# A selective-scan kernel: GpSimd weighs the last token block of 20 of 32 states, TensorE sums them in PSUM, three decay banks

## The chip, the cores and the metric

The kernel runs on one core of a Trainium2 chip. The metric is the device time of one execution in microseconds (us). Matmuls run on TensorE (PE; its weight loads are PEld), scans and sums on VectorE (DVE), table functions and copies out of PSUM on ScalarE (ACT), products in SBUF on GpSimd (POOL), and SyncE (SP) issues the DMAs.

## The reference

Eight sequences of 1024 tokens with 512 features. The result is `x + mamba(layernorm(x)) + ffn(layernorm(x))`; the FFN with its FP4 rounding comes first and is not touched. What matters is the selective scan of the other branch, with 1024 channels d and 16 states s:

```python
def step(h, inp):
    xt, dtt, Bt, Ct = inp
    dA = jnp.exp(dtt[:, :, None] * A[None])
    h = h * dA + (dtt * xt)[:, :, None] * Bt[:, None, :]
    y = jnp.einsum('bds,bs->bd', h, Ct)
    return (h, y)
...
y = y + xc * D_param[None, None, :]
y = y * _silu(z)
return y @ W_out
```

## The kernel before

`phase_b` works through 16 chunks of 512 tokens, two to a sequence; all engines run the same list of slots for every chunk (`over_chunks`), with a hardware loop whose body is two chunks. Channels lie on partitions in two halves of four tiles of 128. A chunk has 32 states k: 0 to 15 are the 16 states of the first half, 16 to 31 those of the second. A state has four tiles j; tile n = 4k + j, 128 to a chunk. I call the time of one state a slot.

For tile n, ScalarE computes the decay exp(dt * A) into the PSUM bank `decay[n % 4]` (L1058), after the scan that read this bank before. GpSimd computes v = u * B into `v[k % 2]` (`drive`, L920), with row B broadcast over partitions by a DMA (`load_b`). VectorE scans along the 512 tokens into `h[k % 2]` (`hs`, L1099). The second chunk of a sequence starts from carried states (`carry`), the first from zero; their scans are listed apart. When the four scans of a state are done, TensorE turns its four blocks t of 128 tokens one after the other so that tokens lie on partitions (`turn_states`, L1216, four transposes of 128 x 128 each into `ht[n % 2]`), and VectorE adds each, times C of its tokens (one number per partition), to `acc[g][:, t, :]` (`add_state`, L1113). TensorE turns tile n in place n + 4 of its list and VectorE adds it in place n + `LAG` = n + 5, so VectorE alternates: scan n, addition n - 5. The first scan of state k waits until state k - 2 is turned, for its buffer.

The rest is spread over the list by hand. `MM` gives the place from which TensorE works on each other product (`ip`, `cv`, `z`, `ssm`, `ct`, `xd`, `yt`, `wo`), 4/3 units a tile; a unit is one K-slice, two matmul instructions of 512 columns. `ACT_AT` gives ScalarE's copies and functions after decay n; the SiLUs need a change of the function table and back (`silu_xc` at 31, 38, 68, 76, `silu_z` at 4 and 87). `DVE_AT` has eight additions of a residual tile (`rtb`, L1085), `POOL_AT` by slot the products y2 = acc * silu(z) (L929) and the last steps of softplus and u = dt * x (`sp`, `du`; L933, L937). `SP_AT` has the DMAs. GpSimd's v of state k goes ahead of the scans by up to two states (it waits for the scan of state k - 2 that read the same buffer). `c_now` is copied once a chunk. Eight PSUM banks are in use: four `decay`, two `ht`, two `mm`.

Of the kernel before, what the change touches and what calls it, by code (L numbers as in the profile page):

```python
# [636 lines left out]
def phase_b(nc, ctx, xnt, res, ssm_d, tap_d, ident, out, W_in, conv_w, conv_b, W_x, A_log, D_param, dt_bias, W_out):  # L637
# [25 lines left out]
    LAG = 5  # L663
    assert ND == 2 * GD and NT == 4 and D == CL and GW == 512 and KC == 4
# [10 lines left out]
    w_in, w_out = sb("w_in", [P, KH, 2 * DI]), sb("w_out", [P, ND, D])  # L675
# [15 lines left out]
    b_rep = [sb(f"b_rep{p}", [P, CL]) for p in range(4)]  # L691
    dt_rep = sb("dt_rep", [P, CL])
# [7 lines left out]
    decay = [psum(f"decay{p}", [P, CL]) for p in range(4)]  # L700
# [16 lines left out]
    b_loaded = [sem(f"b_loaded{p}") for p in range(4)]  # L717
# [17 lines left out]
    for i, part_ in enumerate(MM):  # L735
        for unit in range(UNITS[part_[1]]):
            while room == 0 or place < part_[0]:
# [29 lines left out]
    POOL_AT = {1: [("y2", 1, 0), ("y2", 1, 1)], 2: [("y2", 1, 2), ("y2", 1, 3)],  # L767
# [4 lines left out]
    SP_AT = {2: [("load", 1, 0), ("load", 1, 1)], 5: [("tap", 2)], 7: [("tap", 3)], 8: [("store", 1, 0)],  # L772
             9: [("store", 1, 1), ("load", 1, 2)], 10: [("tap", 4), ("load", 1, 3)], 11: [("tap", 5)], 13: [("store", 1, 2)],
             15: [("store", 1, 3)], 16: [("tap", 6)], 17: [("tap", 7), ("x_in",)], 19: [("tap", 0)],
             20: [("load", 0, 0), ("load", 0, 1)], 21: [("tap", 1)], 23: [("ssm",)], 25: [("store", 0, 0)],
             26: [("store", 0, 1), ("load", 0, 2)], 27: [("load", 0, 3)], 28: [("store", 0, 2)], 29: [("store", 0, 3)],
             31: [("x_z",)]}

# [47 lines left out]
    def _(sp):  # L826
# [24 lines left out]
        sp.dma_start(w_out[:, :, :], W_out.rearrange("(k p) n -> p k n", p=P)).then_inc(w_out_loaded, 16)  # L851
# [8 lines left out]

        def move(c, what, *args):
            o = whose(c, what, *args[:1])
            if what == "tap":
                i, = args
                o = c.plus(1 if i >= 2 else 2)
                if o.exists(NC):
                    load_taps(o, i)
            elif what == "x_in":
# [25 lines left out]
        def part(c):  # L894
            for k in range(SLOTS):
                for what in SP_AT.get(k, ()):
                    move(c, *what)
                if k + 3 < SLOTS:
                    if c.exists(NC):
                        load_b(c, k + 3)  # L900
                elif c.plus(1).exists(NC):
                    load_b(c.plus(1), k + 3 - SLOTS)
# [6 lines left out]
    def _(pool):  # L909
# [11 lines left out]

        def extra(c, what, g, j):
# [3 lines left out]
            if what == "y2":  # L926
                wait(pool, z_ready, o.at(4, 2 * g + j // 2 + 1))
                wait(pool, summed, o.at(128, 64 * g + 61 + j))
# [10 lines left out]
        def part(c):  # L939
            for k in range(SLOTS):  # L940
                if c.exists(NC):
                    drive(c, k)
                for what in POOL_AT.get(k, ()):
                    extra(c, *what)
# [4 lines left out]
    def _(act):  # L949
# [101 lines left out]
        def part(c):  # L1051
            for n in range(4 * SLOTS):
                if c.exists(NC):
                    g, s, j = n // 64, n // 4 % NS, n % 4
                    if s == 0:
                        wait(act, dt_ready, c.at(8, 4 * g + j + 1))
                    wait(act, scanned, c.at(128, n - 3))
                    nc.scalar.activation(decay[n % 4][:, :], dt[g][:, j, :], ACT.Exp,  # L1058
                                         scale=a_neg[:, GD * g + j, s:s + 1]).then_inc(decay_ready, 1)
# [12 lines left out]
    def _(dve):  # L1072
# [15 lines left out]
        def scan(c, n):  # L1088
            g, s, j = n // 64, n // 4 % NS, n % 4
            k = n // 4  # L1090
            if j == 0:
                wait(dve, turned, c.at(128, 4 * (k - 2) + 4))
                if c.second and k < 2:
                    wait(dve, carried, c.in_firsts(32, 2 * NS - 1 + k))
                elif not c.second and k >= 2:
                    wait(dve, carried, c.in_firsts(32, k - 1))
            wait(dve, v_ready, c.at(128, n + 1))
            wait(dve, decay_ready, c.at(128, n + 1))
            nc.vector.tensor_tensor_scan(h[k % 2][:, j, :], decay[n % 4][:, :], v[k % 2][:, j, :],  # L1099
# [3 lines left out]
        def add_state(c, n):  # L1103

            g, s, t = n // 64, n // 4 % NS, n % 4
            if s == 0:
# [3 lines left out]
            else:  # L1110
                wait(dve, summed, c.at(128, n - 3))
            wait(dve, turned, c.at(128, n + 1))
            nc.vector.scalar_tensor_tensor(out=acc[g][:, t, :], in0=ht[n % 2][:, :, :].rearrange("p j d -> p (j d)"),  # L1113
                                           scalar=c_now[:, t, s:s + 1], in1=acc[g][:, t, :],
                                           op0=ALU.mult, op1=ALU.add).then_inc(summed, 1)

        def part(c):
            for n in range(4 * SLOTS):
# [3 lines left out]
                if before.exists(NC):  # L1122
                    add_state(before, m)
                if n == LAG - 1 and c.exists(NC):
                    wait(dve, summed, c.at(128, 0))
# [8 lines left out]
    def _(pe):  # L1134
        pe.wait_ge(w_in_x_loaded, 16)

        def products(c, n, unit):
# [61 lines left out]
            else:  # L1199
                (g, t), j = args, unit  # L1200
                if first:
                    if isinstance(c.q, int) and c.c == 0 and (g, t) == (0, 0):
                        pe.wait_ge(w_out_loaded, 16)
                    wait(pe, yt_copied, o.at(8, 4 * g + t + 1))
                made, done = nc.tensor.matmul(bank[:, :], yt[t % 2][:, j, :], w_out[:, GD * g + j, :],  # L1205
# [4 lines left out]
        def turn_states(c, n):  # L1210

            k, t = n // 4, n % 4
            wait(pe, scanned, c.at(128, 4 * k + 4))
            wait(pe, summed, c.at(128, n - 1))
            for j in range(GD):
                last = nc.tensor.transpose(ht[n % 2][:, j, :], h[k % 2][:, j, t * P:(t + 1) * P], ident[:, :])  # L1216
            last.then_inc(turned, 1)

        def part(c):
            for n in range(4 * SLOTS):  # L1220
                before, m = (c, n - 4) if n >= 4 else (c.plus(-1), n + 4 * SLOTS - 4)
                if before.exists(NC):
                    turn_states(before, m)
                for i, unit in units_at[n]:
# [48 lines left out]
```

## Time and profile before

| | |
|---|---|
| median of 3 runs | 5823.27 us (5817.52 to 5824.12) |
| the profiled execution | 5821.8 us |
| its span, first to last instruction | 5819.3 us |
| PE busy | 4983.0 us (86%) |
| VectorE busy | 5030.1 us (86%) |
| ScalarE busy | 2782.2 us (48%) |
| GpSimd busy | 3629.1 us (62%) |
| chain that ended last, by engine | DVE 30%, PE 13%, issue 13%, ACT 6%, POOL 4% |

Busy shares are over the whole span; the scans begin at 1937.58 us. In the timeline rows the first number is the start in us, the second the length in us, and x is how many equal instructions were merged; square brackets give the idle time ahead and what ended it. The rows of the lines have busy us and mean ns of one.

### The profile page before, as it was taken

What the parts mean: (1) busy time and instruction counts of PE and PEld (TensorE: products, weight loads), DVE (VectorE), ACT (ScalarE), POOL (GpSimd) and SP (SyncE); (2) the same over time, 40 slices, a digit from 0 to 9 for tenths busy, and PEclk for the clock granted to TensorE, in tenths of its full rate; (3) what the DMA queues carried; (4) which work ended last, traced back from release to release, by engine and by line L of the source; (5) the groups of instructions that cost most, each with busy time, mean ns of one, the idle gap of its engine ahead of it and who ended that gap; (6) DMA issues with size and microseconds to landing.
All of it is one profiled execution on the core that took longest, in us unless ns stands there. A gap on an engine that the chain in (4) does not pass through costs nothing.

```text
span 5819.3 us, 78029 instructions
## 1 busy us (share of the span) xinstructions
PE 4983.0 (86%) x21764; PEld 3148.0 (54%) x21764; DVE 5030.1 (86%) x6343; ACT 2782.2 (48%) x4591; POOL 3629.1 (62%) x2810
## 2 busy tenths in 40 slices
PE   1799999999998788888888888888888888888867
PEld 1688888888885344444444444444444444444444
DVE  7667666676662699999999999999999999999998
ACT  1111111111111666666666666666666665666654
POOL 4333333333331687878778788787877878878785
PEclk9999999999999899999999999999999999999968
DMA  2111111111112222222222222222222222222211
GB/s 74 33 40 43 42 41 43 40 43 40 43 40 79 65 78 71 73 73 67 75 71 75 71 65 79 68 75 73 66 74 71 75 70 67 76 71 75 61 57 49
DMA packets 211700, 362.55 MB, mean 62 GB/s; under 512 B 26208, under 2 KB 58976, under 8 KB 207216
## 3 DMA queue, kind: packets, MB, share of 16 engines
q1 hardware_dynamic: 211312, 358.17, 19.8%
q8 instruction: 147, 2.41, 0.2%
q14 instruction: 241, 1.97, 0.1%
HBM read 287.80 MB, written 70.29 MB: 62 GB/s over the span
## 4 chain that ended last, share of the span: by engine, by line
DVE 30%; PE 13%; issue 13%; ACT 6%; POOL 4%; DVEq 1%; DMA 0%; ACTq 0%; SPq 0%; POOLq 0%
DVE hs L1099 18%; DVE acc L1113 11%; PE ht L1216 5%; PE mm L1205 4%; POOL v L920 3%; ACT decay L1058 3%; PE mm L1156 2%; PE mm L1165 2%; DVEq L795 1%; POOL dt L933 1%; DVE rtb L1085 1%; ACT L1067 1%; ACT L983 1%; PE mm L1173 1%; ACT xc L983 1%
## 5 line engine op out<-in xcount | busy, mean ns | idle before, releaser
L920 POOL TENSOR_TENSOR v<-u,b_rep 128x512 f32<-128x512 f32 x2048 | 2578.2, 1273 | 698.0 <-DVE hs L1099 688.6
L1216 PEld LDWEIGHTS ht<-ident,hs 128*128 128x128 f32 x8192 | 957.4, 147 | 1883.7 <-DVE acc L1113 907.1
L1216 PE MATMUL ht<-ident,hs 128*128 128x128 f32 x8192 | 1362.7, 292 | 629.4 <-DVE acc L1113 577.6
L1058 ACT ACTIVATE decay<-dt,a_neg 128x512 f32<-128x512 f32 x2048 | 1377.3, 686 | 600.5 <-DVE hs L1099 575.7
L1113 DVE SCALAR_TENSOR_TENSOR acc<-ht,c_now,acc 128x512 f32<-128x512 f32 x2048 | 1479.9, 723 | 24.0 <-PE ht L1216 23.7
L1099 DVE TENSOR_TENSOR_SCAN hs<-decay,v 128x512 f32<-128x512 f32 x1024 | 1238.3, 1209 | 128.6 <-POOL v L920 105.5
L1099 DVE TENSOR_TENSOR_SCAN hs<-decay,carry,v 128x512 f32<-128x512 f32 x1024 | 1301.3, 1271 | 13.7 <-ACT decay L1058 8.1
L490 ACT ACTIVATE sg<-gate 128x512 f32<-128x512 f32 (+1 forms) x192 | 108.1, 563 | 1334.1 <-PE up L536 1334.1
L1156 PE MATMUL mm<-x_in,w_in 128*128 128x512 f32 x1024 | 526.3, 620 | 20.7 <-DMA x_in<-xnt_d 17.3
L1205 PE MATMUL mm<-w_out,yt 128*128 128x512 f32 x1024 | 537.5, 625 | 0.3 <-ACT yt L1021 0.3
L1173 PE MATMUL mm<-w_in,x_z 128*128 128x512 f32 x1024 | 520.8, 611 | 0.0
L1165 PE MATMUL mm<-xb,tap_diag 128*128 128x512 f32 (+3 forms) x1024 | 501.2, 594 | 2.7 <-ACT xc L978 1.9
L106 POOL TENSOR_TENSOR h<-h,h_small 128x1408 f32<-128x1408 f32 x64 | 166.2, 2597 | 440.3 <-DVE h_small L100 440.3
L151 POOL TENSOR_TENSOR h<-h,h_small 128x1408 f32<-128x1408 f32 x64 | 166.3, 2599 | 335.2 <-DVE h L145 335.2
L435 DVE TENSOR_TENSOR rt<-down,rt 128x512 f32<-128x512 f32 x64 | 44.3, 692 | 323.9 <-PE down L536 323.9
L534 PE MATMUL gate<-gu,xqt 128*128 128x512 f32 (+1 forms) x768 | 301.4, 392 | 5.4 <-DVE xqt L426 5.4
L536 PE MATMUL gate<-gu,xqt 128*128 128x512 f32 (+1 forms) x768 | 289.7, 377 | 0.0
L535 PE MATMUL gate<-gu,xqt 128*128 128x512 f32 (+1 forms) x768 | 289.7, 377 | 0.0
L534 PE MATMUL up<-gu,xqt 128*128 128x512 f32 (+1 forms) x768 | 288.8, 376 | 0.0
L535 PE MATMUL up<-gu,xqt 128*128 128x512 f32 (+1 forms) x768 | 288.6, 376 | 0.0
L536 PE MATMUL up<-gu,xqt 128*128 128x512 f32 (+1 forms) x768 | 288.5, 376 | 0.0
L534 PE MATMUL down<-wd,hqt 128*128 128x512 f32 x704 | 285.1, 405 | 2.5 <-DVE hqt L418 2.5
(122 smaller groups left out, 6948.0 us busy)
## 6 DMA issues: line engine op xcount, KB each, us to landing
b_rep<-ssm_d SPq DMA_DIRECT2D x512, 256.0 KB, 3.4
tap_diag<-tap_d SPq DMA_DIRECT2D x128, 256.0 KB, 3.0
rtb<-res_d SPq DMA_DIRECT2D x128, 256.0 KB, 4.1
xt<-in_L_attn_x SPq DMA_DIRECT2D x64, 256.0 KB, 2.8
xnt_d<-xntb SPq DMA_DIRECT2D x64, 256.0 KB, 2.7
rt<-in_L_attn_x SPq DMA_DIRECT2D x64, 256.0 KB, 2.6
res_d<-rt SPq DMA_DIRECT2D x64, 256.0 KB, 2.0
x_in<-xnt_d SPq DMA_DIRECT2D x16, 1024.0 KB, 4.8
```

What stands on the lines that cost most here:

```text
L534: nc.tensor.matmul(out, left_hi, right_hi, start=(k == 0), stop=False)
L535: nc.tensor.matmul(out, left_hi, right_lo, start=False, stop=False)
L536: last = nc.tensor.matmul(out, left_lo, right_hi, start=False, stop=(k == len(pairs) - 1))
L920: nc.gpsimd.tensor_tensor(v[k % 2][:, j, :], u[g][:, j, :], b_rep[k % 4][:, :], ALU.mult).then_inc(v_ready, 1)
L1058: nc.scalar.activation(decay[n % 4][:, :], dt[g][:, j, :], ACT.Exp, scale=a_neg[:, GD * g + j, s:s + 1]).then_inc(decay_ready, 1)
L1099: nc.vector.tensor_tensor_scan(h[k % 2][:, j, :], decay[n % 4][:, :], v[k % 2][:, j, :], carry[:, s, GD * g + j:GD * g + j + 1] if c.secon ...
L1113: nc.vector.scalar_tensor_tensor(out=acc[g][:, t, :], in0=ht[n % 2][:, :, :].rearrange("p j d -> p (j d)"), scalar=c_now[:, t, s:s + 1], i ...
L1156: made, done = nc.tensor.matmul(bank[:, :], w_in[:, k, i * P:(i + 1) * P], x_in[:, k, :], start=first, stop=last), ip_done
L1165: made, done = nc.tensor.matmul(bank[:, skip:], tap_diag[i % 2][:, tap, :], xb[i % 2][:, tap + skip:tap + CL], start=first, stop=last), cv ...
L1173: made, done = nc.tensor.matmul(bank[:, :], x_z[:, k, t * P:(t + 1) * P], w_in[:, k, DI + g * GW:DI + (g + 1) * GW], start=first, stop=las ...
L1205: made, done = nc.tensor.matmul(bank[:, :], yt[t % 2][:, j, :], w_out[:, GD * g + j, :], start=first, stop=last), wo_done
L1216: last = nc.tensor.transpose(ht[n % 2][:, j, :], h[k % 2][:, j, t * P:(t + 1) * P], ident[:, :])
```

## The change

A set of 20 of the 32 states is `WEIGHED`. For these the last token block (t = 3, `LT`) isn't added by VectorE: GpSimd multiplies the block of `h` by C (row C broadcast by a new DMA, `load_c`) into its own buffer `hw` (`weigh`, after the v of two states later), and TensorE transposes the products into one PSUM bank `yw`, accumulating over the states (`turn_weighed`, two places after where the block was turned). VectorE adds `yw` to the sum once for each half (`add_weighed`), and y2 of the last block waits for it. The bank comes from the decays: three instead of four (`decay_freed` says which scan frees one; the ring begins anew with each chunk). The first scan of state k waits for the weighing of state k - 2 too. For SBUF, `w_out` holds one half and is loaded twice a chunk. GpSimd's other work and the counts of the semaphores are moved accordingly.

```diff
+    LT = NT - 1
+    WEIGHED = (2, 3, 4, 6, 8, 10, 12, 13, 14, 15, 16, 17, 18, 19, 22, 23, 24, 25, 26, 30)
+    LATE = 2
...
-    w_in, w_out = sb("w_in", [P, KH, 2 * DI]), sb("w_out", [P, ND, D])
+    w_in, w_out = sb("w_in", [P, KH, 2 * DI]), sb("w_out", [P, GD, D])
...
+    c_rep = [sb(f"c_rep{p}", [P, P]) for p in range(4)]
+    hw = [sb(f"hw{p}", [P, GD, P]) for p in range(2)]
...
-    decay = [psum(f"decay{p}", [P, CL]) for p in range(4)]
+    decay = [psum(f"decay{p}", [P, CL]) for p in range(3)]
+    yw = psum("yw", [P, GD, P])
...
-    POOL_AT = {1: [("y2", 1, 0), ("y2", 1, 1)], 2: [("y2", 1, 2), ("y2", 1, 3)],
-               6: [("sp", 1, 0), ("du", 1, 0)], 7: [("sp", 1, 1), ("du", 1, 1)], 8: [("sp", 1, 2), ("du", 1, 2)],
-               9: [("sp", 1, 3), ("du", 1, 3)], 22: [("y2", 0, 0), ("y2", 0, 1)], 23: [("y2", 0, 2), ("y2", 0, 3)],
-               29: [("sp", 0, 0), ("du", 0, 0)], 30: [("sp", 0, 1), ("du", 0, 1)],
-               31: [("sp", 0, 2), ("du", 0, 2), ("sp", 0, 3), ("du", 0, 3)]}
-    SP_AT = {2: [("load", 1, 0), ("load", 1, 1)], 5: [("tap", 2)], 7: [("tap", 3)], 8: [("store", 1, 0)],
+    POOL_AT = {2: [("y2", 1, 0), ("y2", 1, 1)], 3: [("y2", 1, 2), ("y2", 1, 3)], 7: [("sp", 1, 0), ("du", 1, 0)],
+               9: [("sp", 1, 1), ("du", 1, 1)], 11: [("sp", 1, 2), ("du", 1, 2)], 13: [("sp", 1, 3), ("du", 1, 3)],
+               22: [("y2", 0, 0), ("y2", 0, 1)], 23: [("y2", 0, 2), ("y2", 0, 3)], 29: [("sp", 0, 0), ("du", 0, 0)],
+               30: [("sp", 0, 1), ("du", 0, 1)], 31: [("sp", 0, 2), ("du", 0, 2), ("sp", 0, 3), ("du", 0, 3)]}
+    SP_AT = {2: [("w_out", 1), ("load", 1, 0), ("load", 1, 1)], 5: [("tap", 2)], 7: [("tap", 3)], 8: [("store", 1, 0)],
...
-             15: [("store", 1, 3)], 16: [("tap", 6)], 17: [("tap", 7), ("x_in",)], 19: [("tap", 0)],
+             15: [("store", 1, 3), ("w_out", 0)], 16: [("tap", 6)], 17: [("tap", 7), ("x_in",)], 19: [("tap", 0)],
...
+    NW = len(WEIGHED)
+    weigh_no = {k: i for i, k in enumerate(WEIGHED)}
+    weighed_until = [sum(k < NS * g for k in WEIGHED) for g in range(3)]
+    add_no = {m: i for i, m in enumerate((k, t) for k in range(SLOTS) for t in range(NT)
+                                         if t != LT or k not in weigh_no)}
+    ADDS = len(add_no)
...
+    def sums(c, k, t):
+        return c.at(ADDS, max(i for (a, b), i in add_no.items() if b == t and a <= k) + 1)
+    def states_done(c, k, of, per):
+        if k < 0:
+            return c.at(per, sum(i <= k + SLOTS for i in of) - per)
+        return c.at(per, sum(i <= k for i in of))
+    def decay_freed(c, n):
+        return c.at(128, n - 2) if n >= 3 else c.at(128, (126, 127, 125)[n] + 1 - 128)
...
-        sp.dma_start(w_out[:, :, :], W_out.rearrange("(k p) n -> p k n", p=P)).then_inc(w_out_loaded, 16)
...
+        def load_c(c, k):
+            w, row = weigh_no[k], k % NS
+            wait(sp, weighed, c.at(NW, w - 3))
+            sp.dma_start(c_rep[w % 4][:, :],
+                         ssm_rows(c, row, row + 1)[:, LT * P:].broadcast_to([P, P])).then_inc(c_loaded[w % 4], 16)
...
         def move(c, what, *args):
...
+            elif what == "w_out":
+                g, = args
+                o = c.plus(-g)
+                if o.exists(NC):
+                    wait(sp, wo_done, o.at(8, 4 * g))
+                    sp.dma_start(w_out[:, :, :], w_out_rows[:, GD * g:GD * g + GD, :]).then_inc(w_out_loaded, 16)
...
+                if c.exists(NC) and k in weigh_no:
+                    load_c(c, k)
...
                         load_b(c, k + 3)
...
+        def weigh(c, k):
+            w = weigh_no[k]
+            wait(pool, c_loaded[w % 4], c.at(4 * NW, 16 * (w // 4) + 16))
+            wait(pool, w_turned, c.at(NW, w - 1))
+            wait(pool, scanned, c.at(128, 4 * k + 4))
+            nc.gpsimd.tensor_tensor(hw[w % 2][:, :, :], h[k % 2][:, :, LT * P:],
+                                    c_rep[w % 4][:, :].unsqueeze(1).broadcast_to([P, GD, P]),
+                                    ALU.mult).then_inc(weighed, 1)
         def extra(c, what, g, j):
...
             if what == "y2":
...
-                wait(pool, summed, o.at(128, 64 * g + 61 + j))
+                if j == LT:
+                    wait(pool, yw_added, o.at(2, g + 1))
+                else:
+                    wait(pool, summed, sums(o, NS * g + NS - 1, j))
                 nc.gpsimd.tensor_tensor(sz[:, j, :], acc[g][:, j, :], sz[:, j, :], ALU.mult).then_inc(y2_ready, 1)
...
                     drive(c, k)
+                done, m = (c, k - 2) if k >= 2 else (c.plus(-1), k + SLOTS - 2)
+                if done.exists(NC) and m in weigh_no:
+                    weigh(done, m)
...
-                    wait(act, scanned, c.at(128, n - 3))
-                    nc.scalar.activation(decay[n % 4][:, :], dt[g][:, j, :], ACT.Exp,
+                    wait(act, scanned, decay_freed(c, n))
+                    nc.scalar.activation(decay[n % 3][:, :], dt[g][:, j, :], ACT.Exp,
                                          scale=a_neg[:, GD * g + j, s:s + 1]).then_inc(decay_ready, 1)
...
             if j == 0:
-                wait(dve, turned, c.at(128, 4 * (k - 2) + 4))
+                wait(dve, turned, states_done(c, k - 2, [i for i, _ in add_no], ADDS))
+                wait(dve, weighed, states_done(c, k - 2, weigh_no, NW))
...
             wait(dve, v_ready, c.at(128, n + 1))
...
-            nc.vector.tensor_tensor_scan(h[k % 2][:, j, :], decay[n % 4][:, :], v[k % 2][:, j, :],
+            nc.vector.tensor_tensor_scan(h[k % 2][:, j, :], decay[n % 3][:, :], v[k % 2][:, j, :],
...
         def add_state(c, n):
...
-            g, s, t = n // 64, n // 4 % NS, n % 4
-            if s == 0:
+            g, s, k, t = n // 64, n // 4 % NS, n // 4, n % 4
+            if s == 0 or (t == LT and all((NS * g + i, t) not in add_no for i in range(s))):
...
-                wait(dve, summed, c.at(128, n - 3))
-            wait(dve, turned, c.at(128, n + 1))
-            nc.vector.scalar_tensor_tensor(out=acc[g][:, t, :], in0=ht[n % 2][:, :, :].rearrange("p j d -> p (j d)"),
+                wait(dve, summed, sums(c, k - 1, t))
+            wait(dve, turned, sums(c, k, t))
+            nc.vector.scalar_tensor_tensor(out=acc[g][:, t, :], in0=ht[add_no[k, t] % 2][:, :, :].rearrange("p j d -> p (j d)"),
...
+        def add_weighed(c, g):
+            wait(dve, w_turned, c.at(NW, weighed_until[g + 1]))
+            wait(dve, summed, sums(c, NS * g + NS - 1, LT))
+            nc.vector.tensor_tensor(acc[g][:, LT, :], yw[:, :, :].rearrange("p j d -> p (j d)"), acc[g][:, LT, :],
+                                    ALU.add).then_inc(yw_added, 1)
...
         def part(c):
...
                     scan(c, n)
-                if before.exists(NC):
+                if before.exists(NC) and (m // 4, m % 4) in add_no:
...
+                for g in range(2):
+                    owner = c if g == 0 else c.plus(-1)
+                    if n == (64 * (g + 1) + LAG + 4) % 128 and owner.exists(NC):
+                        add_weighed(owner, g)
...
-                    wait(dve, summed, c.at(128, 0))
+                    wait(dve, summed, c.at(ADDS, 0))
...
-                    if isinstance(c.q, int) and c.c == 0 and (g, t) == (0, 0):
-                        pe.wait_ge(w_out_loaded, 16)
+                    wait(pe, w_out_loaded, o.at(32, 16 * g + 16))
...
-                made, done = nc.tensor.matmul(bank[:, :], yt[t % 2][:, j, :], w_out[:, GD * g + j, :],
+                made, done = nc.tensor.matmul(bank[:, :], yt[t % 2][:, j, :], w_out[:, j, :],
...
+            if (k, t) not in add_no:
+                return
             wait(pe, scanned, c.at(128, 4 * k + 4))
-            wait(pe, summed, c.at(128, n - 1))
+            wait(pe, summed, c.at(ADDS, add_no[k, t] - 1))
             for j in range(GD):
-                last = nc.tensor.transpose(ht[n % 2][:, j, :], h[k % 2][:, j, t * P:(t + 1) * P], ident[:, :])
+                last = nc.tensor.transpose(ht[add_no[k, t] % 2][:, j, :], h[k % 2][:, j, t * P:(t + 1) * P], ident[:, :])
             last.then_inc(turned, 1)
+        def turn_weighed(c, k):
+            g, w = k // NS, weigh_no[k]
+            wait(pe, weighed, c.at(NW, w + 1))
+            if w == weighed_until[g]:
+                wait(pe, yw_added, c.at(2, g))
+            for j in range(GD):
+                last = nc.tensor.matmul(yw[:, j, :], hw[w % 2][:, j, :], ident[:, :], is_transpose=True,
+                                        start=(w == weighed_until[g] and j == 0),
+                                        stop=(w == weighed_until[g + 1] - 1 and j == GD - 1))
+            last.then_inc(w_turned, 1)
...
         def part(c):
...
                     turn_states(before, m)
+                done, k = (c, n - 7 - LATE) if n >= 7 + LATE else (c.plus(-1), n + 4 * SLOTS - 7 - LATE)
+                if done.exists(NC) and k % 4 == 0 and k // 4 in weigh_no:
+                    turn_weighed(done, k // 4)
...
```

## Rows read from the trace of the kernel before

**Rows 1.** The page: the span.
```profile
span 5819.3 us, 78029 instructions
```

**Rows 2.** Busy us (count) of PE, PEld, DVE, ACT, POOL, clock, DMA in a stretch.
```profile
2647.00:3131.00 484.00, 410.18 (x1712) 214.44 (x1712) 473.45 (x531) 308.70 (x500) 380.90 (x305) 0.97 0.23 72
```

**Rows 3.** Lines of the page.
```profile
L920 POOL TENSOR_TENSOR v<-u,b_rep 128x512 f32<-128x512 f32 x2048 | 2578.2, 1273 | 698.0 <-DVE hs L1099 688.6
...
L1113 DVE SCALAR_TENSOR_TENSOR acc<-ht,c_now,acc 128x512 f32<-128x512 f32 x2048 | 1479.9, 723 | 24.0 <-PE ht L1216 23.7
L1099 DVE TENSOR_TENSOR_SCAN hs<-decay,v 128x512 f32<-128x512 f32 x1024 | 1238.3, 1209 | 128.6 <-POOL v L920 105.5
```

**Rows 4.** Timeline of DVE, a chunk that starts at zero.
```profile
3513.18 1.21 DVE L1099 TENSOR_TENSOR_SCAN hs<-decay,v 128x512 f32<-128x512 f32 x1
3514.31 0.72 DVE L1113 SCALAR_TENSOR_TENSOR acc<-ht,c_now,acc 128x512 f32<-128x512 f32 x1
3514.96 1.21 DVE L1099 TENSOR_TENSOR_SCAN hs<-decay,v 128x512 f32<-128x512 f32 x1
```

**Rows 5.** Timeline of DVE, a chunk with carried states.
```profile
3617.41 1.27 DVE L1099 TENSOR_TENSOR_SCAN hs<-decay,carry,v 128x512 f32<-128x512 f32 x1
...
3619.24 1.27 DVE L1099 TENSOR_TENSOR_SCAN hs<-decay,carry,v 128x512 f32<-128x512 f32 x1
```

**Rows 6.** Timeline around tile 43.
```profile
3457.99 0.68 DVE L1085 TENSOR_TENSOR rtb<-mm,rtb 128x512 f32<-128x512 f32 x1
3457.99 0.72 ACT L1011 ACTIVATE xs<-xc,dpar 128x512 f32<-128x512 f32 x1 [5.13 <-PE mm L1191]
...
3459.39 1.22 DVE L1099 TENSOR_TENSOR_SCAN hs<-decay,v 128x512 f32<-128x512 f32 x1 [0.72 <-ACT decay L1058]
```

**Rows 7.** Waits of DVE from 1937 to 5800: total us, times, longest.
```profile
DVE acc L1113 <- PE ht L1216: 23.7, 14, 3.8
DVE hs L1099 <- ACT decay L1058: 22.6, 28, 1.8
DVE hs L1099 <- PE ht L1216: 13.3, 20, 1.7
DVE rtb L1085 <- PE mm L1205: 12.6, 15, 2.3
```

**Rows 8.** Timeline of the first scans.
```profile
1936.28 9.85 POOL L920 TENSOR_TENSOR v<-u,b_rep 128x512 f32<-128x512 f32 x8
1937.58 6.11 DVE L1099 TENSOR_TENSOR_SCAN hs<-decay,v 128x512 f32<-128x512 f32 x5 [105.49 <-POOL v L920]
```

**Rows 9.** Lines of POOL in the first 1900 us.
```profile
L151 POOL TENSOR_TENSOR xq<-xq,q_small 128x512 f32<-128x512 f32 x64 | 68.0, 1063 | 196.5 <-DVE xq L145 196.5
...
L106 POOL TENSOR_TENSOR w_t<-w_raw,w_small 128x512 f32<-128x512 f32 x22 | 30.4, 1382 | 75.7 <-DVE w_small L130 71.9 <-DVE w_small L100 3.7
```

**Rows 10.** Timeline of PE (matmuls), tiles with one and with two units.
```profile
3522.68 0.60 PE L1216 MATMUL ht<-ident,hs 128*128 128x128 f32 x4
...
3523.98 0.63 PE L1216 MATMUL ht<-ident,hs 128*128 128x128 f32 x4
...
3526.22 1.88 PE L1173 MATMUL mm<-w_in,x_z 128*128 128x512 f32 x4
3527.94 0.60 PE L1216 MATMUL ht<-ident,hs 128*128 128x128 f32 x4
```

**Rows 11.** Timeline from decay 87 to decay 88.
```profile
3532.16 0.69 ACT L1058 ACTIVATE decay<-dt,a_neg 128x512 f32<-128x512 f32 x1 [1.08 <-DVE hs L1099]
...
3535.90 2.50 POOL L929 TENSOR_TENSOR sz<-acc,sz 128x512 f32<-128x512 f32 x2 [2.44 <-ACT sz L1000]
...
3538.09 2.53 ACT L1058 ACTIVATE decay<-dt,a_neg 128x512 f32<-128x512 f32 x4
```

**Rows 12.** DMA issues: count, KB each, median us to landing.
```profile
b_rep<-ssm_d SPq DMA_DIRECT2D x512, 256.0 KB, 3.4
...
w_out<-in_L_attn_W_out SPq DMA_DIRECT2D x1, 2048.0 KB, 19.9
```

More of the change, by code:

```diff
@@ L716, in phase_b @@
     rt_loaded, rt_stored = ([sem(f"{s}{p}") for p in range(2)] for s in ("rtb_loaded", "rtb_stored"))
-    b_loaded = [sem(f"b_loaded{p}") for p in range(4)]
+    b_loaded, c_loaded = ([sem(f"{s}_loaded{p}") for p in range(4)] for s in "bc")
+    weighed, w_turned, yw_added = sem("weighed"), sem("w_turned"), sem("yw_added")
     v_ready, decay_ready, scanned, turned, summed, carried = (
@@ L777, in phase_b @@
              31: [("x_z",)]}
+    NW = len(WEIGHED)
[4 more added lines that the diff above has]
+    ADDS = len(add_no)
+    assert ADDS % 2 == 0 and NW % 4 == 0
+    def sums(c, k, t):
[6 more added lines that the diff above has]
+        return c.at(128, n - 2) if n >= 3 else c.at(128, (126, 127, 125)[n] + 1 - 128)
     def bank_of(*task):
@@ L850, in _ @@
         sp.dma_start(w_in[:, :, DI:2 * DI], w_in_rows[:, :, DI:2 * DI]).then_inc(w_in_z_loaded, 16)
-        sp.dma_start(w_out[:, :, :], W_out.rearrange("(k p) n -> p k n", p=P)).then_inc(w_out_loaded, 16)
+        w_out_rows = W_out.rearrange("(k p) n -> p k n", p=P)
         def load_b(c, k):
```

## The prediction

> **What bounds the kernel now.** Read the span first [rows 1], then a stretch of the steady phase [rows 2], the table of lines [rows 3], VectorE's timeline [rows 4 to 6] and last its waits [rows 7]. The first 1937.6 us of the span are the FFN and the first projections, and the change does not touch them. From there VectorE runs 2048 scans and 2048 additions. In 484 us of this phase (one pair of chunks) it is busy for 473.45, GpSimd for 380.90, and TensorE's clock is granted at 0.97 of its upper level, 2.4 GHz [rows 2]. The timeline says what a tile costs on VectorE: a scan starts 1.13 us before the addition behind it, the next scan 0.65 us after that; each overlaps the end of the one ahead by 0.08 us [rows 4]. So a tile takes 1.77 us in a chunk that starts at zero and 1.83 us in one that starts from carried states [rows 4, 5]. Per chunk that is 128 x 1.77 = 226.6 or 128 x 1.83 = 234.2 us. The eight additions of a residual take 0.60 each (0.68 less the overlap [rows 6]) and the copy of C 0.7, so 232.1 and 239.7; eight of each are 3774 us. VectorE's waits after the first scan add 23.7 + 22.6 + 13.3 + 12.6 = 72.2 us [rows 7]. With the first 1937.6 us and a tail of 26 us this gives 5810, 0.2% off the span of 5819.3 [rows 1]. **VectorE's own work is the path, and a VectorE instruction that disappears is worth its pitch, not its busy time.**
>
> **Part by part.** The sum is made against the profiled execution, 5821.8 us; the median of the runs is 1.5 us above it, and I add that at the end. Tile n is 4k + j of state k, a slot is the time of one state.
>
> *Removed: 20 of 128 additions a chunk.* An addition is 723 ns busy [rows 3] but its pitch between two scans is 1.77 - 1.13 = 0.64 us. 320 of them: **-204.8 us**, if a scan behind a scan starts after 1.13 us as an addition does. The trace has scans in a row only at the very start: five in 6.11 us, a pitch of 1.225, while GpSimd delivered their inputs at (9.85 - 1.26) / 7 = 1.227 [rows 8]; they were paced by GpSimd, so the pitch lies between 1.13 and 1.22. I take 1.13, because every other VectorE instruction here overlaps its forerunner; the other end costs 320 x 0.08 = 26 us and stays in the range.
>
> *Added on VectorE: one addition of the bank yw to each half's sum.* 32 x 0.60 (priced as the residual's addition [rows 6]) = **+19.2 us**. It waits for the last accumulating transpose, two tiles back, and GpSimd's y2 of the last block waits for it; that y2 sits a state behind, so neither is late.
>
> *Moved to GpSimd: 20 products a chunk.* Price between 1.06 us (a product with a broadcast operand) and 1.38 us [rows 9]; I take 1.27, the line next to it on the same data [rows 3]. GpSimd's busy time per chunk goes from 190.5 to 190.5 + 25.4 = 215.9 us against some 233 for VectorE. A weighed slot has five GpSimd operations at a pitch of 1.23 to 1.24, 6.2 us, against VectorE's 3 x 1.77 + 1.13 = 6.44. A product can end 2.0 us after the start of a slot at the earliest (its state's last scan ends, one v, the product) and is due when the next slot starts, so GpSimd may be 4.4 us late. The slots with two softplus or y2 operations take 7.5 us against 7.1; the last has four of them and takes 10. From slot 24 (0.8 us before due) over 25 to 31 this goes -1.6, -1.9, -2.7, -3.5, -2.5, -2.1, +0.8, and the one due at the next chunk's start is met by 0.1 us. Nothing in the sum, but no room either. One rule speaks against such a move: the Trainium skill, GPSIMD Engine Reference, section Engine selection, puts elementwise work on VectorE, since GpSimd is about twice as slow with two inputs. The rows say 1.27 against 0.72, 1.8 times; by the page's factor the product would be 1.44 us and GpSimd's chunk 219 us, still under VectorE's.
>
> *TensorE.* As many transposes as before (80 a chunk accumulate into yw, two tiles later). A tile with one product unit takes 1.30 us, with two 1.72 + 0.44 = 2.16 [rows 10], on average 1.59; VectorE's weighed tile is 6.44 / 4 = 1.61. TensorE may be late by 2.0 us against VectorE before an addition waits. It nearly becomes a second bound; 0.5 us a chunk for jitter. Against that, a scan of state k that waited for the last transpose of state k - 2 is now released one tile earlier where that state is weighed (states 0, 25 and 26, where most of these waits lie): **-10** of the 13.3 us [rows 7].
>
> *Three decay banks.* ScalarE may be two tiles and a bit ahead instead of three: it loses one pitch, 1.77 us, of cover wherever it stops for long. Its longest stop is the SiLU of z with two table loads at tile 87: decay 87 starts at 3532.16, decay 88 ends at 3538.09 + 0.63, 6.6 us later [rows 11]. With four banks the start is the end of scan 83; with three, the end of scan 84, and scan 88 is due 3 x 1.77 + 1.13 - 1.21 = 5.2 us after that: 1.4 us late. The same shift delays y2, which idles 2.44 us there already [rows 11]; that is in the slack above. 1.45 and 1.25 us in the two kinds of chunk, **+21.6**. The other stops with table loads are 3.9 us; in weighed slots 3.7 are covered: +0.4 in the even chunks, +3. At tile 43 a scan already waits 0.72 us for a decay behind a copy that waits for TensorE [rows 6]; the accumulating transposes of state 8 come one tile ahead of it (0.44) and the tile before is shorter: +0.8 a chunk, **+13**. At a chunk's start the ring begins anew, and decays 0 and 1 may start only after scans 126 and 127: ready 0.8 us later, due 2.3 us later. ScalarE's other copies wait for TensorE and come three tiles behind it, which three banks still allow.
>
> *SyncE's queue.* 20 rows of C a chunk, issued two slots ahead (13 us) against 3.4 us for a row of B; half of W_out twice a chunk, issued 2.3 slots (15 us) ahead, where all of it took 19.9 us once [rows 12]. Each stands ahead of B rows that have three slots. Hidden; if a C row were late it would hold GpSimd and, within 4.4 us, every scan.
>
> Sum: -204.8 + 19.2 - 10 + 21.6 + 3 + 13 + 8 (jitter) = -150. 5821.8 - 150 = 5671.8; plus 1.5: **5673 us**.
>
> **Rivals.** (1) *Scans in a row at 1.21 us:* +26, 5699; chance 0.12. (2) *GpSimd becomes the bound:* it decides once GpSimd has more than 233 - 216 = 17 us of idle a chunk that it can't make up (before, it idled for 51, nearly all on scans). For: no spare in slots 24 to 31 and a y2 that waits for ScalarE. Against: each step above meets its date. With 20 us of such idle, 3 x 16 = +48: 5721; chance 0.09. (3) *TensorE becomes the bound in weighed slots:* from a mean of 1.61 us a tile. At 1.65, 0.04 x 4 x 320 = +51: 5724; chance 0.09. (4) *Slower: the ring of decays.* Each place where ScalarE stops pays the full lost pitch, 1.77 us, on VectorE. The gain without ScalarE's terms is 196 us, 12.2 a chunk, so it decides from seven such places; ScalarE has six table blocks and some thirty copies that wait for TensorE, and with ten paid places the time is 5823 - 196 + 283 = 5910. For: ScalarE is busy for 309 of 484 us [rows 2] and a bank is its only cover. Against: scans waited for decays only 28 times, 22.6 us in all [rows 7]. Chance 0.07, and 0.01 for a smaller loss. (5) *The change does nothing:* the bank can't be summed in time and the stalls meet the gain; 5823, chance 0.03.
>
> **How the numbers follow.** The forecast has 0.59. Its own bounds: nothing new stalls, -204.8 + 19.2 - 13.3 = -199, 5624; all stalls twice as dear, 5720. Rivals 1 to 3 reach 5750 with the longer scan pitch on top, so the range is 5620 to 5750. What a measurement here can tell from no change is 0.2%, 12 us. Faster 0.59 + 0.12 + 0.09 + 0.09 = 0.89, same 0.03, slower 0.08.
>
> **What would show it.** VectorE's group of additions 1728 instead of 2048 at 723 ns, its busy time down by 26 us in a pair of chunks; scans in a row 1.13 apart; waits on decays up from 22.6 to about 55 to 60 us, most at tile 88; waits on transposes at a state's first scan down to a few us; no wait on products of GpSimd. If scans wait for v or the weighed buffer, rival 2; if additions wait for transposes in slots 14 to 21, rival 3; if waits on decays pass 150 us, rival 4. The prediction is wrong if a pair of chunks takes less than 458 or more than 476 us.

## The result and the profile after

| | before | after |
|---|---|---|
| median of the runs | 5821.25 us | 5686.77 us (5684.53 to 5689.05) |
| ratio | | 0.9768, 95% interval 0.9757 to 0.978 |
| span of the profiled execution | 5819.3 us | 5684.8 us |
| VectorE busy | 5030.1 us | 4871.6 us |
| GpSimd busy | 3629.1 us | 3984.9 us |

The change takes 134.5 us off the span, 2.3% of the time. The forecast was 5673 us in a range of 5620 to 5750; the gain was forecast at 150 us. From the second pair of chunks on, a pair takes 466 to 470 us, within the 458 to 476 us that the prediction gave.

The lines of the page that answer to [rows 1] and [rows 3], busy us and mean ns of one, then the idle time ahead:

```profile
span 5684.8 us, 79958 instructions
...
L963 POOL TENSOR_TENSOR v<-u,b_rep 128x512 f32<-128x512 f32 x2048 | 2555.2, 1274 | 201.9 <-DVE hs L1159 188.0
...
L1159 DVE TENSOR_TENSOR_SCAN hs<-decay,v 128x512 f32<-128x512 f32 x1024 | 1232.3, 1216 | 152.3 <-POOL v L963 108.4
L1159 DVE TENSOR_TENSOR_SCAN hs<-decay,carry,v 128x512 f32<-128x512 f32 x1024 | 1293.3, 1275 | 26.7 <-ACT decay L1117 17.5
L1173 DVE SCALAR_TENSOR_TENSOR acc<-ht,c_now,acc 128x512 f32<-128x512 f32 x1728 | 1262.1, 730 | 11.9 <-PE ht L1288 11.4
...
L971 POOL TENSOR_TENSOR hw<-hs,c_rep 128x512 f32<-128x512 f32 x320 | 407.7, 1274 | 6.2 <-DVE hs L1159 6.2
```

There are 320 additions less, and GpSimd has 320 products at 1274 ns, the price of v. Its idle time ahead of v fell from 698 us to 202: the slack went into the products. From the list of all lines, the new addition of yw and the copy of C:

```profile
L1181 DVE TENSOR_TENSOR acc<-yw,acc 128x512 f32<-128x512 f32 x32 | 21.8, 681 | 0.1
...
L1198 DVE COPY c_now<-c_next 128x64 f32<-128x64 f32 x16 | 39.9, 2494 | 1.6
```

The second row is the surprise. This copy was there before, and its sixteen took 10.8 us in all; its row of before, and of after, as min/median/max ns:

```profile
L1127 DVE COPY c_now<-c_next x16: 168/718/1351, 1943.6 to 5557.5; 128x64 f32<-128x64 f32 x16
```
```profile
L1198 DVE COPY c_now<-c_next x16: 170/2624/3759, 1941.5 to 5434.3; 128x64 f32<-128x64 f32 x16
```

The same stretch as [rows 2] (busy us of PE, PEld, DVE, ACT, POOL, clock, DMA) and VectorE's waits after the first scan. As in [rows 7], the last four additions of a residual, in the final 20 us, are left out:

```profile
2647.00:3131.00 484.00, 413.58 (x1777) 227.11 (x1775) 471.06 (x512) 325.32 (x519) 442.00 (x358) 0.98 0.28 88
```
```profile
DVE hs L1159 <- ACT decay L1117: 43.7, 39, 1.8
DVE hs L1159 <- PE ht L1288: 18.7, 17, 1.6
DVE rtb L1144 <- PE mm L1275: 16.8, 19, 2.3
DVE acc L1173 <- PE ht L1288: 11.4, 21, 1.0
DVE hs L1159 <- POOL hw L971: 5.8, 4, 1.9
DVE hs L1159 <- issue: 2.2, 1, 2.2
DVE hs L1159 <- POOL v L963: 1.6, 1, 1.6
```

VectorE is the path as before; GpSimd is busy for 442 of 484 us instead of 381. The waits sum to 100.2 us against 72.2. The account of the span: removed additions 320 x 0.64 = -204.8; yw +19.2; the copy of C 39.9 us now against 10.8, +29; waits +28.0; the first scan 2.1 us earlier (1935.48). That makes -130.6 of the measured -134.5; the last 4 us stay without a name.

### The profile page after: what moved, and what is told of

It is laid out like the page before. It is cut to its first block, busy times and chain, and to the rows that moved or that the text cites. A ratio compares the mean times of both kernels' runs of the same rounds, so it can differ in the third digit from the quotient of the medians.

```text
span 5684.8 us, 79958 instructions
## 1 busy us (share of the span) xinstructions
PE 4886.1 (86%) x21764; PEld 3186.2 (56%) x21764; DVE 4871.6 (86%) x6055; ACT 2821.3 (50%) x4591; POOL 3984.9 (70%) x3130
## 3 DMA queue, kind: packets, MB, share of 16 engines
q8 instruction: 142, 2.33, 0.2%
## 4 chain that ended last, share of the span: by engine, by line
DVE 23%; issue 18%; POOL 11%; PE 7%; ACT 7%; DVEq 1%; DMA 0%; POOLq 0%; ACTq 0%; SPq 0%
DVE hs L1159 14%; POOL v L963 8%; DVE acc L1173 8%; ACT decay L1117 3%; PE mm L1275 2%; PE ht L1288 2%; PE mm L1227 1%; DVEq L823 1%; POOL dt L989 1%; POOL sz L985 1%; ACT L1042 1%; POOL hw L971 1%; ACT xc L1042 1%; DVE rtb L1144 1%; PE mm L1244 1%
## 5 line engine op out<-in xcount | busy, mean ns | idle before, releaser
L963 POOL TENSOR_TENSOR v<-u,b_rep 128x512 f32<-128x512 f32 x2048 | 2555.2, 1274 | 201.9 <-DVE hs L1159 188.0
L1117 ACT ACTIVATE decay<-dt,a_neg 128x512 f32<-128x512 f32 x2048 | 1399.5, 688 | 1061.0 <-DVE hs L1159 1033.6
L1288 PEld LDWEIGHTS ht<-ident,hs 128*128 128x128 f32 x6912 | 827.8, 146 | 1503.4 <-issue 629.3
L1288 PE MATMUL ht<-ident,hs 128*128 128x128 f32 x6912 | 1127.5, 288 | 500.8 <-DVE acc L1173 318.6
L1173 DVE SCALAR_TENSOR_TENSOR acc<-ht,c_now,acc 128x512 f32<-128x512 f32 x1728 | 1262.1, 730 | 11.9 <-PE ht L1288 11.4
L1275 PE MATMUL mm<-w_out,yt 128*128 128x512 f32 x1024 | 517.2, 612 | 43.5 <-ACT xb L1027 26.4
L1244 PE MATMUL mm<-w_in,x_z 128*128 128x512 f32 x1024 | 507.0, 603 | 0.0
L971 POOL TENSOR_TENSOR hw<-hs,c_rep 128x512 f32<-128x512 f32 x320 | 407.7, 1274 | 6.2 <-DVE hs L1159 6.2
```

Of the source, the lines that this page charges most:

```text
L963: nc.gpsimd.tensor_tensor(v[k % 2][:, j, :], u[g][:, j, :], b_rep[k % 4][:, :], ALU.mult).then_inc(v_ready, 1)
L1117: nc.scalar.activation(decay[n % 3][:, :], dt[g][:, j, :], ACT.Exp, scale=a_neg[:, GD * g + j, s:s + 1]).then_inc(decay_ready, 1)
L1173: nc.vector.scalar_tensor_tensor(out=acc[g][:, t, :], in0=ht[add_no[k, t] % 2][:, :, :].rearrange("p j d -> p (j d)"), scalar=c_now[:, t, ...
L1244: made, done = nc.tensor.matmul(bank[:, :], x_z[:, k, t * P:(t + 1) * P], w_in[:, k, DI + g * GW:DI + (g + 1) * GW], start=first, stop=las ...
L1288: last = nc.tensor.transpose(ht[add_no[k, t] % 2][:, j, :], h[k % 2][:, j, t * P:(t + 1) * P], ident[:, :])
```

## The experiments

Times are medians of four or more runs, each beside runs of the kernel before on the same chip (5820.8 to 5824.6 us). The chips differ by up to 4 us, and the four runs of one kernel lie 5 to 12 us apart, so a difference of a few us between two experiments says nothing.

**The copy of C.** In the timeline of the changed kernel (start, length) the copy lies beside GpSimd's work like this:

```profile
3095.74 0.73 DVE L1173 SCALAR_TENSOR_TENSOR acc<-ht,c_now,acc 128x512 f32<-128x512 f32 x1
...
3096.58 2.50 POOL L985 TENSOR_TENSOR sz<-acc,sz 128x512 f32<-128x512 f32 x2
3096.59 3.76 DVE L1198 COPY c_now<-c_next 128x64 f32<-128x64 f32 x1
...
3099.03 1.26 POOL L963 TENSOR_TENSOR v<-u,b_rep 128x512 f32<-128x512 f32 x1
...
3100.27 1.27 DVE L1159 TENSOR_TENSOR_SCAN hs<-decay,carry,v 128x512 f32<-128x512 f32 x1
```

A copy of 64 columns takes 3.76 us; it begins with three GpSimd instructions and ends 0.06 us after the third. What GpSimd does next is this:

```profile
3101.62 1.27 POOL L963 TENSOR_TENSOR v<-u,b_rep 128x512 f32<-128x512 f32 x1 [1.32 <-DVE hs L1159]
```

It stands still until the scan behind the copy is done. 14 of the 16 copies end like this one, 0.05 us after the last instruction that GpSimd had before such a stop; 9 of the 16 last through at least two instructions that GpSimd began after them. In the kernel before, one took 0.81 us beside a running v and ended 0.05 us after it; there 15 of 16 ended with the one GpSimd instruction that was running when they began, and GpSimd went on without a stop. The first experiment keeps place and data and changes only the instruction.

```diff
-                    nc.vector.tensor_copy(c_now[:, :, :], c_next[:, :, :]).then_inc(c_set, 1)
+                    nc.vector.tensor_reduce(c_now[:, :, :].rearrange("p t s -> p (t s)"),
+                        c_next[:, :, :].rearrange("p t s -> p (t s)").unsqueeze(2), AX.X, ALU.max).then_inc(c_set, 1)
```

> The changed kernel, only the copy of C on VectorE written as a tensor_reduce over an axis of length 1 (same data, same place in the list). In the changed kernel this copy takes 2.6 us in the median and up to 3.8, against 0.7 before. Theory A (the copy holds or waits for the SBUF interface that VectorE and GpSimd share, and a reduce does not need it): the instruction takes 0.3 us or less, 16 x 2.4 = 38 us less at most, 5687 falls to about 5655 as part of it turns up as another wait. Theory B (any VectorE instruction at this place is slow, or scan 5 has to wait for its decay anyway): no change, 5687 within 5 us.

Measured: 5662.5 us (ratio to before 0.9728, 0.9712 to 0.9745), 24 us under the changed kernel; of the 36 us that the instruction itself lost, some 7 came back as other waits of VectorE (106.9 us against 100.2).

```profile
L1198 DVE TENSOR_REDUCE c_now<-c_next x16: 194/220/222, 1940.7 to 5405.9; 128x64 f32<-128x64 f32 x16
```

All sixteen take 0.19 to 0.22 us, also where GpSimd's multiplications start beside them. So not the place but the kind of instruction is slow there. What separates the kinds is stated by the Trainium skill, SBUF — State Buffer, section Who interferes with whom: a `tensor_copy` can enter a mode that takes the port pair which VectorE shares with GpSimd, and one of the two then blocks, while `tensor_reduce` never does on this chip. The trace agrees for the reduce, and for the copy in that it ends only when an instruction of GpSimd has ended. What the rows show beyond it is that the copy can be passed over by one or two further GpSimd instructions that began after it; why, and the ports themselves, no run here shows.

**No copy at all.**

```diff
-    c_now, c_next = sb("c_now", [P, NT, NS]), sb("c_next", [P, NT, NS])
+    c_of = [sb(f"c_of{p}", [P, NT, NS]) for p in range(2)]
...
-                    wait(act, c_set, o.at(1, 0))
+                    wait(act, summed, o.at(ADDS, -ADDS))
-                    nc.scalar.activation(c_next[:, :, :], mm
+                    nc.scalar.activation(c_of[o.second][:, :, :], mm
...
-                    nc.vector.tensor_copy(c_now[:, :, :], c_next[:, :, :]).then_inc(c_set, 1)
...
```

> The changed kernel without the copy of C: ScalarE writes C of alternate chunks into two tiles, VectorE reads them there. Theory A: like the reduce and another 0.2 us a chunk, 5650. Theory B (scan 5 waits for decay 5 behind the SiLU of z, or for GpSimd's v): the 2.6 us come back as a wait of scan 5, 5682 or more.

Measured: 5649.0 us (0.9707, 0.9691 to 0.9724), 37.8 us under the changed kernel, where the copies took 39.9 us. Next to nothing took the copy's place; it was path, and almost in full.

**The removal alone.**

```diff
-    decay = [psum(f"decay{p}", [P, CL]) for p in range(3)]
-    yw = psum("yw", [P, GD, P])
+    decay = [psum(f"decay{p}", [P, CL]) for p in range(4)]
...
-                    load_c(c, k)
-                    weigh(done, m)
-                        add_weighed(owner, g)
-                    turn_weighed(done, k // 4)
...
```

> Only the removal: the 320 additions of the last block are left out, and nothing does their work (no products on GpSimd, no rows of C, no accumulating transposes, no addition of yw), with four decay banks. The blocks are missing in the sums. My sum for the removal alone: 320 x 0.64 = 205 us less and most of the 13 us of scans that waited for transposes, 5821 - 205 - 10 = 5606. If a scan behind a scan starts after 1.21 us, 5632. If TensorE were the bound as soon as VectorE is faster, not under 5640.

This kernel leaves the blocks out of the sums, so it is a measure of time only. Measured: 5602.7 us (0.9621, 0.9605 to 0.9638), 218 us under before where the sum says 215. A scan behind a scan is not paced at 1.21: in the changed kernel two in a row show as

```profile
1961.72 2.33 DVE L1159 TENSOR_TENSOR_SCAN hs<-decay,v 128x512 f32<-128x512 f32 x2
...
3087.15 2.47 DVE L1159 TENSOR_TENSOR_SCAN hs<-decay,carry,v 128x512 f32<-128x512 f32 x2
```

that is 2.33 - 1.21 = 1.12 us apart. With carried states it is 2.47 - 1.27 = 1.20. Over all pairs of the changed kernel without a wait between them the medians are 1.13 us (147 pairs) and 1.19 us (152 pairs), the same as from a scan to an addition.

That 218 lies so close to 215 is partly luck. VectorE's waits fell by 24 us, from 72.2 to 48.4, and not by 10, and this run has a copy of C that grew too:

```profile
L1181 DVE COPY c_now<-c_next x16: 170/1720/3337, 1944.4 to 5355.0; 128x64 f32<-128x64 f32 x16
```

These sixteen take 28.2 us, 17 us more than before, with not one product of C on GpSimd. What this kernel shares with the changed one is the new list of GpSimd's other work (`POOL_AT`), in which the products y2 stand later, and there too most of the copies stand beside y2. In e4_three_banks, which has the old list, the sixteen take 11.5 us. So more than half of the copy's +29 us needs no added load on GpSimd at all. Whether the moved products y2 do it, or VectorE's shorter list, isn't settled, as no run moved y2 alone.

**Three decay banks alone**, in the kernel before.

```diff
-    decay = [psum(f"decay{p}", [P, CL]) for p in range(4)]
+    decay = [psum(f"decay{p}", [P, CL]) for p in range(3)]
...
-                    wait(act, scanned, c.at(128, n - 3))
+                    wait(act, scanned, c.at(128, n - 2) if n >= 3 else c.at(128, (126, 127, 125)[n] + 1 - 128))
```

> The kernel before with three decay banks instead of four and nothing else. By the sum of the prediction, without short slots: decay 88 is ready 6.6 us after the end of scan 84 and scan 88 is due 5.9 us after it (even chunks) or 6.1 (odd): 0.75 and 0.5 us, 10 us in all, 5831. The rival of the ring (every stop of ScalarE pays 1.77 us): +150 us or more.

Measured: 5829.2 us, +8.4 (ratio 1.0013, 1.0003 to 1.0023). The wait is where it was put, at tile 88 (this row is of a chunk that starts at zero; with carried states it is 0.52). The sixteen of them sum to 10.7 us:

```profile
4031.32 1.22 DVE L1099 TENSOR_TENSOR_SCAN hs<-decay,v 128x512 f32<-128x512 f32 x1 [0.80 <-ACT decay L1058]
```

0.75 and 0.5 were expected. In the list of all waits those for decays grow by only 1.1 us, because the first scan of the loop body (two chunks) waited 6.9 us for decays before and waits under other names here. In the changed kernel, where the slot is short, the same wait is

```profile
3250.53 1.28 DVE L1159 TENSOR_TENSOR_SCAN hs<-decay,carry,v 128x512 f32<-128x512 f32 x1 [1.18 <-ACT decay L1117]
...
3955.03 1.22 DVE L1159 TENSOR_TENSOR_SCAN hs<-decay,v 128x512 f32<-128x512 f32 x1 [1.46 <-ACT decay L1117]
```

against a forecast of 1.25 and 1.45. Rival 4, every stop of ScalarE at full price, would have cost 150 us or more; it falls.

**The wait at tile 43**, on the kernel without the copy. In the changed kernel it is

```profile
3875.82 0.69 DVE L1144 TENSOR_TENSOR rtb<-mm,rtb 128x512 f32<-128x512 f32 x1 [1.11 <-PE mm L1275]
3878.15 1.22 DVE L1159 TENSOR_TENSOR_SCAN hs<-decay,v 128x512 f32<-128x512 f32 x1 [1.64 <-ACT decay L1117]
```

twice what [rows 6] show. In the chunks that start at zero the wait grew by 0.8 us as forecast (0.86 to 1.66 in the mean), in the others by 0.4 (0.73 to 1.15). In this chunk the residual's addition ahead of it waits for TensorE too.

```diff
-              ... 42: [("xs", 1, 3)], 45: [("xd", 1, 1)],
+              ... 44: [("xs", 1, 3)], 45: [("xd", 1, 1)],
```

> The kernel without the copy of C (5649 us), and ScalarE's scaled copy xs(1, 3), which waits for a transpose that TensorE does in place 42, stands behind decay 44 instead of decay 42. In e2_nocopy the scan of tile 43 starts 1.7 us late in even chunks and 1.5 in odd ones, waiting for its decay. If the copy ahead of decay 43 is the cause: this stall goes, 16 x 1.6 = 26 us, 5623. If TensorE is what holds the stretch back (then the addition of the residual or a transpose is late next): less than 8 us, 5641 or more.

Measured: 5628.1 us (0.9663, 0.9647 to 0.9679), 20.9 us less than without the edit, of 26. VectorE's waits for decays fall from 48.3 to 30.2 us; those for TensorE's products rise from 14.8 to 17.9.

**The stop at tile 87 cut in two.**

```diff
-              81: [("z", 0, 2)], 87: [("z", 0, 3), ("silu_z", 0, 0), ("silu_z", 0, 1)], 92
+              81: [("z", 0, 2)], 83: [("silu_z", 0, 0)], 84: [("z", 0, 3)], 87: [("silu_z", 0, 1)], 92
```

> The kernel without the copy of C (5649 us), and ScalarE's stop of 5.1 us at tile 87 (copy of z, table load, two SiLUs, table load) cut in two: one SiLU with its table loads (3.6 us) behind decay 83, the copy behind decay 84, the other SiLU (3.6 us) behind decay 87. Theory of the ring (three banks cover 3.7 us in a weighed slot): the waits at tile 88, 1.55 and 1.28 us a chunk, go, 16 x 1.42 = 23 us, 5626, though ScalarE does 2.6 us more work a chunk. If the wait at tile 88 were TensorE's (transposes of state 20 behind the ssm products): no more than half of it, 5638.

Measured: 5636.9 us (0.9676, 0.9659 to 0.9692), 12.1 us less, about half. By the time alone this could also be the rival of the expectation (no more than half, 5638 us), so the rows have to tell. With carried states the wait for the decay is gone. In chunks that start at zero 0.85 us remain in four of the eight, and in the other four the scan waits 0.6 us for a transpose:

```profile
3918.24 1.28 ACT L1059 ACT_TABLE_LOAD   x1
...
3923.01 1.90 ACT L1117 ACTIVATE decay<-dt,a_neg 128x512 f32<-128x512 f32 x3
...
3925.06 1.28 ACT L1059 ACT_TABLE_LOAD   x1
...
3928.73 1.91 ACT L1117 ACTIVATE decay<-dt,a_neg 128x512 f32<-128x512 f32 x3
```
```profile
3930.08 1.22 DVE L1159 TENSOR_TENSOR_SCAN hs<-decay,v 128x512 f32<-128x512 f32 x1 [0.85 <-ACT decay L1117]
```

After the first stop ScalarE catches up with three decays in a row and goes straight into the second: two stops four tiles apart add up. My bound of 3.7 us supposes a ScalarE that starts punctually, and it doesn't here. Of the 5.8 us left at tile 88 in these chunks, TensorE has 2.4, and 3.2 us of waits for decays are new at tile 116.

**Both, and no copy.**

> Both edits and no copy of C: 5649 - 26 - 23 = 5600 if the three causes are separate stalls of VectorE. If they share a cause (TensorE is late anyway and one wait covers the other), 5620 or more.

Measured: 5609.6 us (0.9629, 0.9613 to 0.9646), 39.4 us under the kernel without the copy, where the two edits alone gave 20.9 + 12.1. They are separate stalls; the 6 us more are within the scatter of the runs. VectorE's waits for decays are down to 6.5 us; those of scans for transposes went up from 14.6 to 27.1. Of this rise 7.9 us are at tile 88, where the decay was late before: TensorE is next there. Another 6.0 us are at the first scan of the loop body, where VectorE waits about 15 us in all, in this kernel as in the kernel without the copy (14), and the trace names now one engine, now another.

**Four states more on GpSimd.**

```diff
-    WEIGHED = (2, 3, 4, 6, 8, 10, 12, 13, 14, 15, 16, 17, 18, 19, 22, 23, 24, 25, 26, 30)
+    WEIGHED = (2, 3, 4, 5, 6, 7, 8, 9, 10, 12, 13, 14, 15, 16, 17, 18, 19, 22, 23, 24, 25, 26, 30, 31)
```

> As e7_all, with four states more weighed (5, 7, 9 and 31: 24 of 32). VectorE's list is 4 x 16 x 0.64 = 41 us shorter. GpSimd has 176 operations a chunk at 1.24, 218 us of about 225, and in slots 7, 9 and 11 seven of them, 8.7 us against 6.4: by the sum of the prediction it is past its 4.4 us of slack in slot 11 by about 1 us. If VectorE is the bound: 5600 - 41 + 16 = 5575. If GpSimd is the bound by now: 5600 or more, and scans wait for v or for the weighed buffer by more than 60 us.

Measured: 5592.6 us (0.9605, 0.9589 to 0.9621), 17 us less of 41 removed, between the 5575 of the one theory and the 5600 of the other. Its stretch of 484 us:

```profile
2647.00:3131.00 484.00, 422.59 (x1828) 234.78 (x1828) 473.04 (x516) 339.26 (x535) 464.60 (x377) 0.97 0.29 93
```

GpSimd is busy for 464.6 of 484 us and VectorE for 473; the two are level. Yet scans wait for v 15.4 us and for the weighed buffer 0.9 us, not the 60 of the rival; and 12.5 of the 15.4 us are at the first scan of the loop body, where e7_all waits as long under other names. So VectorE is still the longer list. What grew against e7_all are the waits for decays (17.9 us against 6.5, of which 9.1 are at tile 5) and those of residual additions (20.6 against 14.0).

**Two residual additions one place later**, on top.

```diff
-    DVE_AT = {21: [("add", 1, 0)], 29: [("add", 1, 1)], 42: [("add", 1, 2)], 50: ...
+    DVE_AT = {21: [("add", 1, 0)], 30: [("add", 1, 1)], 43: [("add", 1, 2)], 50: ...
```

> As e8_24_states, with two of VectorE's residual additions one place later in its list (tiles 30 and 43 instead of 29 and 42). In e8 such an addition waits 0.9 us for the product that TensorE ends in the same place; all waits of residual additions are 34.8 us, of which some 14 lie in the tail. If these waits are only a matter of order: 21 us less at most, 5593 falls to about 5577. If TensorE is late in this stretch whatever VectorE does (transposes are then late instead), or if its next product but one waits for the bank that is freed later: no gain, 5588 or more.

Measured: 5575.0 us (0.9575, 0.9559 to 0.9591), 17.6 us less. Their wait is gone from the list of waits, and transposes took part of it over (additions that wait for them: 19.2 us against 11.7). With the same idea as the change, this kernel is 4.2% under before instead of 2.3%, and 2% under the changed one.

## Why the prediction was right, point by point

- **VectorE's list is the path, and an instruction is worth its pitch.** Held, by the starts in the timeline: 0.64 us from an addition to the next scan, before and after. The removal alone gave -218 us against -215, but this total proves less than it seems to, as two errors in it cancel in part (waits -24 for -10, copy of C +17 for nothing).
- **A scan behind a scan starts after 1.13 us.** Held (1.13 in the median, 1.19 with carried states); rival 1 falls.
- **The bank yw, +19.2 us.** 21.8 us busy at 681 ns less the overlap of 0.08: 19.2. Held. That its reader is never late did not hold: GpSimd's y2 of the last block waits for this addition 15 times, 35.2 us in all, between the first scans and 5560 us. It cost slack of GpSimd and no more, as VectorE waited for GpSimd only 7.4 us.
- **GpSimd's products are hidden at 1.27 us.** Price held (1274 ns), and scans wait for hw 5.8 us and for v 1.6 us. All of the 5.8 us are at the first scan of the loop body, where GpSimd itself started 2.5 to 2.7 us late by its "issue" waits, and where the same scan waited 6.9 us for its decay before. Rival 2 falls. But "nothing in the sum" was wrong by another road, next.
- **The failed step: nothing was charged for what GpSimd's new list does to VectorE's other instructions.** I priced the copy of C at 0.7 us from the trace of before and left it there. In the changed kernel it took 2.5 us in the mean: +29 us. e1_reduce and e2_nocopy show that this is the copy and its kind. It looks like the price of a fuller GpSimd, but e3_removed, with 28.2 us of copies and no product added, shows that the added load is not needed for more than half of it. Rows of before gave the hint: 168 ns at the least and 1351 at the most for the same 64 columns.
- **Scans released earlier by weighed states, -10 us.** Failed: 13.3 became 18.7. The waits at states 26 and 27 are gone, but I had misplaced the others; they lie at the first scan of state 1, which waits for state 31, and 31 is not weighed. In e8_24_states, where it is, no scan of state 1 waits for a transpose any more (9.4 us in e7_all). But there 9.1 us of waits for decays stand one tile later, so it is open whether weighing state 31 would have saved the time.
- **Three banks.** Held closely: tile 88 1.46 and 1.18 us (1.45 and 1.25 forecast); tile 43 +9.8 us in all of the 13 forecast; tile 69 0.16 us, in the chunks that start at zero only. All waits for decays rose by 21.1 us to 43.7, not to 55 to 60: 9.0 us of before, at the first scans of states 0 and 1, now stand under other names. In exchange additions wait 11.4 us for transposes instead of 23.7; before, 21.6 of these were at the start of the loop body.
- **TensorE nearly a second bound.** It cost little here (residual additions 16.8 against 12.6 us) and shows once the rest is gone, at tile 88 in e7_all.
- **The sum.** Waits were forecast at +35.6 and are +28.0; the copy is +29 for which I had nothing. By these two the gain would be 129 instead of 150; the earlier first scan (2 us) and the 4 us without a name bring it to 134.5. That the time lies only 14 us over the forecast owes something to luck: the waits came out 8 us lower, for reasons that the sum did not have.

## What to carry to other kernels

Take an instruction on the bounding engine at its pitch, and cost a shared resource as a bank or a lookahead at the few places where the engine behind it stops for long; here the pitch was right to 0.01 us, and the two waits at the longest stop to 0.1 us. When GpSimd's list changes, look at every short copy on VectorE whose minimum and maximum lie far apart: it waits for whatever GpSimd runs beside it, and another form of instruction or a second buffer frees it. After such a move the order written by hand is tuned for the old pace, and three edits of places alone gave 51 us beside the change's 134.

## What the runs showed that I had not expected

A VectorE copy of 64 columns took 0.17 us at its shortest, when GpSimd's instruction was just ending. Its median was 0.7 us in the kernel before (GpSimd busy for 381 of 484 us), 1.7 us in e3_removed (403 of 484, no product added), and 2.6 us, up to 3.76, in the changed kernel (442 of 484). The same data through a reduce took 0.19 to 0.22 us each time. Apart from the shortest ones, the copies of all these kernels end 0.05 to 0.06 us after the end of a GpSimd instruction. What decides how many of them a copy waits for isn't shown: the load, the kind of instruction beside it (nearly always v before, mostly y2 after) and whether GpSimd is about to stop all changed at once, and none was set by hand.
